# A recurrent attention layer with a gated FFN: the first step's order on four engines, and where the state's products stand in the loop

## The chip, the cores and the metric

The kernel runs on one core of a Trainium2 chip. The metric is the device time of one execution in microseconds (us). The kernel before was run three times: 142.39, 144.08 and 145.32 us, median 144.08 us. A further execution was taken with the profiler; it took 140.76 us, and its span on the core, from the first instruction to the last, is 139.0 us.

## What is computed

For `x` of 4 sequences x 512 tokens x 256 features, with 16 heads of 16:

```
xn   = layernorm(x)
q,k,v = silu(xn Wq), silu(xn Wk), silu(xn Wv)
per head, in chunks:  S_new = chunk_decay * S + (k * k_decay)^T v
                      o     = (q k^T * D) v + (q S) * q_decay
gate = (xn Wg1) Wg2
o    = rmsnorm_per_head(o * sigmoid(gate)) * norm_w
s    = o Wo
g    = silu(fp8(xn * scale) fp8(W2 * scale1) / (scale * scale1))
out  = x + s * g
```

`D` is the causal decay mask. The rounding to 8 bits is done by arithmetic: a magic number derived from the exponent is added and subtracted (`e4_magic`, `e4_sum`, `e4_q`), and values that are too large are turned into NaN by way of PSUM (`find_over`, `put_nan`). W2 goes through the same steps once: `w2_y` (scaled), `w2_m` (exponent), `w2_f32` (magic), `w2_m` (sum), `w2_q`, `w2_over`, `w2_fp8`.

## The kernel before, in words

**Tiling.** The 2048 tokens are worked in 8 steps (`STEPS`). A step `n` takes one tile of 128 tokens from each of two sequences (`S = 2`), so 256 tokens. Steps alternate between two pairs of sequences (`PAIRS = 2`), so the state that step `n` reads was made in step `n - 2`, and steps 0 and 1 begin with a state of zero. A tile of 128 tokens is two chunks of 64 (`c = 0, 1`): `state_mid` is the state between them, `state_end` the state after both. The last two steps make no `state_end`.

**Engines.** Each engine has its own list of instructions, written out by hand, and runs it in order; semaphores tie the lists together. TensorE (PE) has the products, ScalarE (ACT) the silu and tanh functions and copies, VectorE (DVE) the masks, the norms and the states, GpSimd (POOL) the decays and the rounding, SyncE (SP) issues all DMAs. There is no planner: the order in each list is the schedule.

**One step of the loop on PE**, in order (`for n in range(1, STEPS - 1)`, from L1227): `scores(n)` (L1052, 64 small products into `b_s` and `b_o`), `head_sums(n-1)` (L1140), `project_q(n+1)` (L956, L961), `project_g1`, `project_k` and `project_v` of `n+1` (L969 to L998), `spread_rs(n-1)` (L1148), `state_steps(n)` (L1075, 64 products of 64x32: what both chunks add to the state), `gate(n+1)` (L1006), `from_chunk(n,0,0)` (L1116, 32 products), `transpose_x(n+2)`, `from_chunk(n,0,1)`, `transpose_k(n+1)`, `project_o(n-1,0)` (L1164), `from_chunk(n,1,0)`, `from_state(n,0)` and `from_state(n,1)` (L1097, 32 products of 32x32 each: what the state gives to the first and to the second chunk), `ffn(n+1)` (L1023), `from_chunk(n,1,1)`, `project_o(n-1,1)`. The pieces named L1052, L1075, L1097 and L1116 use a part of the array per product (the profile shows it as 32*64, 64*32, 32*32); the others use 128 rows.

**PSUM.** The banks are shared. `ps_u[0]`, where `state_steps` puts the first chunk's share, is in `b_q`; `ps_u[1]`, the second's, is in k's bank `b_k`. `b_o` holds two of the four blocks of scores and then the attention output. `b_v` holds v, and `g1` and `ps_spread` in turn.

**Waits around the change.** `scores(n)` waits for `s_ffn` (the silu of the FFN product of `n`), `s_gate` and `s_og` (`gate_o(n-1)` on DVE, L710). `gate(n+1)` waits for all four masks of step `n` (`mask`, L677). `project_o(n-1,0)` waits for the two states of step `n`. `transpose_k(n+1)` waits for `state_end`.

**The start.** Step 0 stands ahead of the loop in every list. On ACT: ... `silu_q(1)`, `silu_q_parity(1)`, `silu_k(1)`, `normalise(2)`, `silu_v(1)`, `gate(0)`, `high_g1(1)`, `w2_over`, `copy_kT(1)`, `gate(1)`, `find_over(1)`, `high_xT(2)`, `scale_y(2)`, `silu_ffn(0)`, `square_o(0)`, `silu_ffn(1)`. On DVE, near its end: `add_state_mid(0)`, `add_state_end(0)`, `w2_q`, `low_g1(1)`, `head_sum`, `w2_fp8`, `put_nan(1)`, `gate_o(0)`, `low_xT(2)`, `head_spread`, `stats(3)`. POOL scales W2 (L429) and makes its sum (L436).

## Time and profile before

| what | value |
|---|---|
| median of 3 runs | 144.08 us (142.39 to 145.32) |
| the profiled execution | 140.76 us |
| its span | 139.0 us |
| PE busy | 123.4 us, 89% of the span |
| DVE, ACT, POOL busy | 103.3, 75.9, 72.3 us |
| share of PE in the chain that ended last | 66% |

Busy time is the sum over an engine's instructions. A wait says who sat idle before an instruction and what ended it; "issue" means that nothing in the profile explains the idle time. The chain of waits is followed back from the last instruction of all. In the line PEclk each digit is the TensorE clock that was granted in one fortieth of the span, in tenths of full speed.

### The profile page before, as it was taken

What the parts mean: (1) busy time and instruction counts of PE and PEld (TensorE: products, weight loads), DVE (VectorE), ACT (ScalarE), POOL (GpSimd) and SP (SyncE); (2) the same over time, 40 slices, a digit from 0 to 9 for tenths busy, and PEclk for the clock granted to TensorE, in tenths of its full rate; (3) what the DMA queues carried; (4) which work ended last, traced back from release to release, by engine and by line L of the source; (5) the groups of instructions that cost most, each with busy time, mean ns of one, the idle gap of its engine ahead of it and who ended that gap; (6) DMA issues with size and microseconds to landing.
All of it is one profiled execution on the core that took longest, in us unless ns stands there. A gap on an engine that the chain in (4) does not pass through costs nothing.

```text
span 139.0 us, 7207 instructions
## 1 busy us (share of the span) xinstructions
PE 123.4 (89%) x3130; PEld 104.0 (75%) x3130; DVE 103.3 (74%) x276; ACT 75.9 (55%) x143; POOL 72.3 (52%) x112
## 2 busy tenths in 40 slices
PE   3999897945999999999997998999999999887890
PEld 3989895814997799779975896779887987566660
DVE  0899997992888499849990999279937990597963
ACT  7689779829166646664664486365663572104000
POOL 6708999948237186707671584438442842400030
PEclk9999999997799999999999999999999999999999
DMA  2959400000000000100020002000200020020004
GB/s 81 270 155 366 142 0 7 5 0 9 0 0 5 5 5 23 57 5 5 10 73 5 5 0 80 5 5 5 78 5 5 5 78 5 5 80 5 5 0 151
DMA packets 6848, 6.06 MB, mean 44 GB/s; under 512 B 1377, under 2 KB 6817, under 8 KB 6817
## 3 DMA queue, kind: packets, MB, share of 16 engines
q1 hardware_dynamic: 6816, 5.60, 12.6%
q8 instruction: 25, 0.41, 1.2%
q14 instruction: 7, 0.05, 0.1%
HBM read 3.50 MB, written 2.10 MB: 40 GB/s over the span
## 4 chain that ended last, share of the span: by engine, by line
PE 66%; DVE 12%; POOL 10%; issue 8%; ACT 2%; POOLq 0%; DVEq 0%; ACTq 0%
PE b_q L1164 8%; PE b_o L1116 7%; PE b_q L956 5%; PE b_s L1052 4%; PE b_o L1097 4%; PE b_kv L970 4%; PE b_kv L969 4%; PE b_kv L972 4%; PE b_kv L1033 3%; PE b_s L1023 2%; PE b_q L1075 2%; PE b_o L1052 2%; PE b_x L942 2%; PE b_q L961 2%; PE b_s L1006 2%
## 5 line engine op out<-in xcount | busy, mean ns | idle before, releaser
L351 POOL TENSOR_TENSOR e_sum<-e_y,e_magic 128x512 f32<-128x512 f32 x8 | 10.3, 1281 | 19.0 <-DVE e_magic L662 19.0
L710 DVE SCALAR_TENSOR_TENSOR og<-gate_tanh,b_o 128x512 f32<-128x512 f32 x7 | 4.8, 687 | 17.6 <-PE b_o L1116 17.6
L969 PE MATMUL b_kv<-w_hi,xT_hi 128*128 128x256 f32 x64 | 16.6, 281 | 0.0
L970 PE MATMUL b_kv<-w_lo,xT_hi 128*128 128x256 f32 x64 | 16.4, 280 | 0.0
L389 POOL TENSOR_TENSOR y<-sg,x_sb 128x512 f32<-128x512 f32 x7 | 9.0, 1292 | 13.2 <-DVE sg L779 13.2
L1116 PE MATMUL b_o<-probs,v_par 64*32 64x64 f32 x896 | 13.6, 223 | 1.7 <-issue 1.6
L1116 PEld LDWEIGHTS b_o<-probs,v_par 64*32 64x32 f32 x896 | 8.9, 106 | 7.4 <-issue 6.3
L677 DVE TENSOR_TENSOR probs<-b_o,decay_mask 128x512 f32<-128x512 f32 x16 | 10.3, 685 | 4.3 <-PE b_o L1052 4.1
L361 POOL TENSOR_TENSOR qd<-q_silu,q_decay 128x512 f32<-128x512 f32 x8 | 10.4, 1302 | 5.4 <-ACT q_silu L487 5.4
L1164 PE MATMUL b_q<-wo_scaled,on 128*128 128x256 f32 x48 | 13.0, 392 | 0.0
L1052 PE MATMUL b_s<-q_par,kT 32*64 32x128 f32 x256 | 10.1, 293 | 3.1 <-issue 3.1
L972 PE MATMUL b_kv<-w_hi,xT_lo 128*128 128x256 f32 x64 | 12.7, 279 | 0.0
L487 ACT ACTIVATE q_silu<-b_q 128x512 f32<-128x512 f32 x8 | 4.8, 602 | 13.6 <-PE b_q L961 12.9
L1052 PEld LDWEIGHTS b_s<-q_par,kT 32*64 32x64 f32 x256 | 8.1, 139 | 5.5 <-issue 5.4
L969 PEld LDWEIGHTS b_kv<-w_hi,xT_hi 128*128 128x128 f32 x64 | 12.0, 188 | 0.2 <-issue 0.2
L970 PEld LDWEIGHTS b_kv<-w_lo,xT_hi 128*128 128x128 f32 x64 | 12.0, 188 | 0.0
L371 POOL TENSOR_TENSOR own_mid<-state_mid,head_parity 128x128 f32<-128x128 f32 x8 | 3.7, 458 | 15.5 <-DVE state_mid L690 12.8
L1052 PE MATMUL b_o<-q_par,kT 32*64 32x128 f32 x256 | 10.6, 295 | 0.7 <-issue 0.7
L356 POOL TENSOR_TENSOR e_q<-e_sum,e_magic 128x512 bf16<-128x512 f32 x8 | 10.3, 1290 | 0.6
L482 ACT ACTIVATE e_y<-b_x,scales 128x512 f32<-128x512 f32 x8 | 5.5, 689 | 8.8 <-DVE xT_lo L653 8.8
L677 DVE TENSOR_TENSOR probs<-b_s,decay_mask 128x512 f32<-128x512 f32 x16 | 10.2, 680 | 0.0
L492 ACT ACTIVATE q_par<-b_q,head_parity 128x512 f32<-128x512 f32 x16 | 10.1, 688 | 0.0
(184 smaller groups left out, 353.4 us busy)
## 6 DMA issues: line engine op xcount, KB each, us to landing
out_dram<-y SPq DMA_DIRECT2D x7, 256.0 KB, 2.2
x_sb<-in_L_attn_x_dram SPq DMA_DIRECT2D x4, 384.0 KB, 5.7
x_sb<-in_L_attn_x_dram SPq DMA_DIRECT2D x2, 256.0 KB, 3.5
w_f<-in_L_attn_Wq_dram SPq DMA_DIRECT2D x1, 256.0 KB, 3.6
w_f<-in_L_attn_Wk_dram SPq DMA_DIRECT2D x1, 256.0 KB, 3.8
w_f<-in_L_attn_Wv_dram SPq DMA_DIRECT2D x1, 256.0 KB, 4.7
w_f<-in_L_ffn_input_dram SPq DMA_DIRECT2D x1, 256.0 KB, 3.7
wo_f<-in_L_attn_Wo_dram SPq DMA_DIRECT2D x1, 256.0 KB, 6.1
```

Of the source, the lines that this page charges most:

```text
L351: g.tensor_tensor(e4_sum[:], e4_y[:, n % 2], e4_magic[:, n % 2], ALU.add).then_inc(s_e4sum, 1)
L356: g.tensor_tensor(e4_q[:], e4_sum[:], e4_magic[:, n % 2], ALU.subtract).then_inc(s_e4q, 1)
L361: g.tensor_tensor(qd[:, n % 2].rearrange("p k (s t) -> p k s t", s=S), q_silu[:].rearrange("p k (s t) -> p k s t", s=S), q_decay[:].unsque ...
L389: g.tensor_tensor(y[:, n % 2], sg[:, n % 2].rearrange("p (s d) -> p s d", s=S), x_sb[:, x_tiles(n), :], ALU.add).then_inc(s_y, 1)
L492: a.activation(q_par[:, n % 2, par], ps_q, ACT.Silu, scale=head_parity[:, par:par + 1]).then_inc(s_qpar, 1)
L677: v.tensor_tensor(probs[:, r], ps_score[r].rearrange("p (s z) -> p s z", s=S), decay_mask[:, r].unsqueeze(1).broadcast_to([P, S, 4 * C]), ...
L969: t.matmul(dst[:, s], xT_hi[:, u, kk, tok], w_hi[:, w, kk], start=(s == 0 and kk == 0), stop=False, skip_group_check=True)
L970: t.matmul(dst[:, s], xT_hi[:, u, kk, tok], w_lo[:, w, kk], start=False, stop=False, skip_group_check=True)
L972: mm = t.matmul(dst[:, s], xT_lo[:, u, kk, tok], w_hi[:, w, kk], start=False, stop=(kk == KH - 1), skip_group_check=True)
L1052: mm = t.matmul(ps_score[r][c * C:c * C + C, cols], kT[rows, u, half, tok], q_par[rows, u, :, half, tok], start=True, stop=True, skip_grou ...
L1116: mm = t.matmul(dst[32 * r:32 * r + 32, c, z:z + C], v_par[rows, u, blk:blk + 2 * E], probs[rows, r, s, i:i + C], start=(half == 0 and s = ...
L1164: mm = t.matmul(dst, on[:, n % 2, kk, s * P:s * P + P], wo_scaled[:, kk], start=(kk == 0 and (s == 0 or n == STEPS - 1)), stop=(kk == KH - ...
```

## The change

The change has three parts.

1. **The start.** The scaling of W2 moves from POOL to ACT (between `normalise(1)` and `silu_q(0)`), its sum from POOL to DVE. `head_parity` and `own_block` are made at the very start of DVE's list, `head_sum` a little later; the memsets of `wg1_a` and `wg1_b` move behind `lag_logdecay`. SP waits for a lower count before it loads Wg2 and W2. On ACT `silu_q_parity(1)` goes ahead of `silu_q(1)` and `silu_v(1)` ahead of `normalise(2)`. On POOL `decay_k(0)` goes behind the rounding, and `decay_q(1)`, `decay_k(1)` wait for `w2_fp8`. On PE the two FFN products are exchanged: `ffn(1)` comes ahead of `from_chunk(0,1,1)` and `ffn(0)` behind it; ACT takes `silu_ffn(1)` ahead of `scale_y(2)` and `silu_ffn(0)` after `square_o(0)`. `scores(1)` waits for the first of the two only. On DVE `add_state_end(0)`, `stats(3)` and `low_xT(2)` now stand between `put_nan(1)` and `gate_o(0)`.
2. **The state's steps.** `state_steps(n)` is cut in two calls of 32 products. The first, `c = 0`, stays in its place. The second, `c = 1`, comes behind `transpose_x(n+2)`, writes to v's bank `b_v` instead of `b_k`, waits for `silu_v(n+1)`, and stands where `from_chunk(n,0,1)` stood; that one and `transpose_k(n+1)` come behind `project_o(n-1,0)`. `project_g1` now waits for `state_end`, `transpose_k` and `project_o` no longer do.
3. **The state's share.** `from_state(n,0)` goes between `project_k(n+1,0)` and `project_k(n+1,1)`, waits for the first mask, and begins the sum in the bank's first half; `from_state(n,1)` stays.

Before the last step, `state_steps(7)` moves ahead of `from_chunk(6,1,1)`.

```diff
@@ -160,7 +160,7 @@
 ps_ffn0 = b_q[:].rearrange("p (s n) -> p s n", s=S)
-ps_u = [b[:, 0:W // 4].rearrange("p (k s e) -> p k s e", k=KH, s=S) for b in (b_q, b_k)]
+ps_u = [b[:, 0:W // 4].rearrange("p (k s e) -> p k s e", k=KH, s=S) for b in (b_q, b_v)]
 ps_k = b_k[:].rearrange("p (s n) -> p s n", s=S)
...
@@ -413,34 +415,34 @@
 pool.wait_ge(s_pool, 11)
-g.memset(wg1_a[:].bitcast(F32), 0.0).then_inc(s_pool, 1)
-g.memset(wg1_b[:].bitcast(F32), 0.0).then_inc(s_pool, 1)
 g.memset(head_sum[:], 0.0).then_inc(s_pool, 1)
...
 g.memset(minus_third[:], 0.0).then_inc(s_pool, 1)
-pool.wait_ge(s_pool, 16)
+pool.wait_ge(s_pool, 14)
 g.memset(minus_third[64:96], -1.0).then_inc(s_pool, 1)
+pool.wait_ge(s_pool, 15)
+pool.wait_ge(s_laglog, 1)
+g.memset(wg1_a[:].bitcast(F32), 0.0).then_inc(s_pool, 1)
+g.memset(wg1_b[:].bitcast(F32), 0.0).then_inc(s_pool, 1)
 pool.wait_ge(s_pool, 17)
 norm_factors(1)
-pool.wait_ge(s_w2, 16)
-pool.wait_ge(s_scale[1], 16)
-g.tensor_scalar(w2_y[:], w2_f32[:], scales[:, 1:2], None, ALU.mult).then_inc(s_w2q, 1)
-decay_k(0)
 sum_y(0)
 round_y(0)
+decay_k(0)
 decay_q(0)
 norm_factors(2)
-pool.wait_ge(s_w2q, 3)
-g.tensor_tensor(w2_m[:], w2_y[:], w2_f32[:], ALU.add).then_inc(s_w2sum, 1)
 sum_y(1)
-pool.wait_ge(s_dvec, 4)
+pool.wait_ge(s_hpar, 2)
 own_state_mid(0)
 round_y(1)
-own_state_end(0)
+pool.wait_ge(s_w2q, 6)
 decay_q(1)
 decay_k(1)
+own_state_end(0)
 norm_factors(3)
@@ -524,7 +526,8 @@
 def silu_ffn(n):
-    act.wait_ge(s_ffnps, n + 1)
+    act.wait_ge(s_ffnps, 2 - n if n < 2 else n + 1)
     need(act, s_sg, n - 2)
...
@@ -574,21 +577,25 @@
 normalise(1)
+act.wait_ge(s_w2, 16)
+act.wait_ge(s_scale[1], 16)
+a.activation(w2_y[:], w2_f32[:], ACT.Copy, scale=scales[:, 1:2]).then_inc(s_w2q, 1)
 silu_q(0)
-act.wait_ge(s_wg2, 64)
-a.activation(wg2_hi[:], wg2_f32[:], ACT.Copy).then_inc(s_g2w, 1)
 act.wait_ge(s_vzero, 2)
...
 high_g1(0)
+act.wait_ge(s_wg2, 64)
+a.activation(wg2_hi[:], wg2_f32[:], ACT.Copy).then_inc(s_g2w, 1)
 scale_y(1)
 find_over(0)
+act.wait_ge(s_qps, 2)
+silu_q_parity(1)
 silu_q(1)
-silu_q_parity(1)
 silu_k(1)
+silu_v(1)
 normalise(2)
-silu_v(1)
 gate(0)
@@ -597,11 +604,11 @@
 high_xT(2)
+act.wait_ge(s_dvec, 4)
+silu_ffn(1)
 scale_y(2)
-act.wait_ge(s_dvec, 6)
+square_o(0)
 silu_ffn(0)
-square_o(0)
-silu_ffn(1)
 act.wait_ge(s_wo, 48)
...
@@ -695,6 +703,7 @@
     p = pair(n)
+    dve.wait_ge(s_u[1], n + 1)
     dve.wait_ge(s_mid, mids(n))
...
@@ -783,9 +792,14 @@
+dve.wait_ge(s_pool, 9)
+v.tensor_reduce(head_parity[:, 0:1], own_head[:].rearrange("p (a b) -> p a b", b=2)[:, :, 0], AX_X, ALU.add).then_inc(s_hpar, 1)
+v.tensor_tensor(own_block[:], own_head[:].rearrange("p (a b) -> p a b", b=2)[:, :, 0],
+                own_head[:].rearrange("p (a b) -> p a b", b=2)[:, :, 1], ALU.add)
+dve.wait_ge(s_hpar, 1)
+v.tensor_scalar(head_parity[:, 1:2], head_parity[:, 0:1], -1.0, 1.0, ALU.mult, ALU.add).then_inc(s_hpar, 1)
 stats(0)
 dve.wait_ge(s_ld, 16)
-dve.wait_ge(s_pool, 9)
 for half in range(KH):
@@ -797,6 +811,11 @@
 v.tensor_scalar(not_ahead[:], lag[:], 0.0, None, ALU.is_ge).then_inc(s_ahead, 1)
+dve.wait_ge(s_pool, 12)
+for half in range(KH):
+    hs = v.tensor_scalar(head_sum[:, half].rearrange("p (j z) -> p j z", j=8)[:, :, half * HH:half * HH + HH],
+                         own_head[:].unsqueeze(1).broadcast_to([P, 8, HH]), 0.5, None, ALU.mult)
+hs.then_inc(s_hsum, 1)
 dve.wait_ge(s_w[0], 16)
...
@@ -837,41 +851,39 @@
     mask(0, r)
+dve.wait_ge(s_w2q, 1)
+v.tensor_scalar(w2_m[:].bitcast(I32), w2_y[:].bitcast(I32), 0x7F800000, None, ALU.bitwise_and).then_inc(s_w2q, 1)
 low_xT(1)
...
 dve.wait_ge(s_g2w, 1)
-dve.wait_ge(s_pool, 17)
+dve.wait_ge(s_pool, 15)
 v.scalar_tensor_tensor(out=wg2_stack[:], in0=wg2_hi[:].bitcast(F32), scalar=minus_third[:, 0:1], in1=wg2_f32[:],
...
 magic(1)
-dve.wait_ge(s_w2q, 1)
-v.tensor_scalar(w2_m[:].bitcast(I32), w2_y[:].bitcast(I32), 0x7F800000, None, ALU.bitwise_and).then_inc(s_w2q, 1)
 dve.wait_ge(s_w2q, 2)
 v.tensor_scalar(w2_f32[:], w2_m[:], E4_MIN, E4_MAGIC, ALU.max, ALU.mult).then_inc(s_w2q, 1)
+dve.wait_ge(s_w2q, 3)
+v.tensor_tensor(w2_m[:], w2_y[:], w2_f32[:], ALU.add).then_inc(s_w2sum, 1)
 put_nan(0)
 add_state_mid(0)
-add_state_end(0)
 dve.wait_ge(s_w2sum, 1)
...
 v.reciprocal(inv_scales[:], scales[:]).then_inc(s_dvec, 1)
-for half in range(KH):
-    hs = v.tensor_scalar(head_sum[:, half].rearrange("p (j z) -> p j z", j=8)[:, :, half * HH:half * HH + HH],
-                         own_head[:].unsqueeze(1).broadcast_to([P, 8, HH]), 0.5, None, ALU.mult)
-hs.then_inc(s_hsum, 1)
-dve.wait_ge(s_dvec, 5)
+dve.wait_ge(s_dvec, 3)
 v.tensor_scalar(descale[:], inv_scales[:, 0:1], inv_scales[:, 1:2], None, ALU.mult).then_inc(s_dvec, 1)
...
 put_nan(1)
+add_state_end(0)
+stats(3)
+low_xT(2)
 gate_o(0)
-low_xT(2)
 dve.wait_ge(s_pec, 1)
 v.tensor_scalar(head_spread[:], ps_spread, -0.75, None, ALU.mult).then_inc(s_dvec, 1)
-stats(3)
 exponent(2)
@@ -888,8 +900,8 @@
     add_state_mid(n)
+    put_nan(n + 1)
     add_state_end(n)
-    put_nan(n + 1)
     if known(n + 3):
@@ -949,7 +961,7 @@
-        pe.wait_ge(s_ffn, 1)
+        pe.wait_ge(s_ffn, 2)
     for part in (w_hi, w_lo):
@@ -990,8 +1002,11 @@
     pe.wait_ge(s_v, n if n > 1 else n + 1)
+    if n > 1:
+        pe.wait_ge(s_end, min(n - 1, STEPS - PAIRS))
     if n == 2:
-        pe.wait_ge(s_dvec, 7)
+        pe.wait_ge(s_dvec, 5)
     for kk in range(KH):
...
@@ -1026,8 +1041,6 @@
     pe.wait_ge(s_k, n + 1)
-    need(pe, s_end, min(n, STEPS - PAIRS))
     for s in range(S):
@@ -1039,7 +1052,7 @@
     if n > 0:
-        pe.wait_ge(s_ffn, n + 1 if n < STEPS - 1 else n)
+        pe.wait_ge(s_ffn, 1 if n == 1 else n + 1 if n < STEPS - 1 else n)
         pe.wait_ge(s_gate, n + 1)
@@ -1053,28 +1066,32 @@
-def state_steps(n):
+def state_steps(n, c):
     u = n % 2
+    if c == 1 and pos(n) == NB - 1:
+        return
     pe.wait_ge(s_kd, n + 1)
     pe.wait_ge(s_v, n + 1)
-    pe.wait_ge(s_kT, n + 1)
     if known(n + 1):
-        pe.wait_ge(s_k, n + 2)
-        pe.wait_ge(s_qpar, 2 * (n + 2))
+        if c == 0:
+            pe.wait_ge(s_q, n + 2)
+            pe.wait_ge(s_qpar, 2 * (n + 2))
+        else:
+            pe.wait_ge(s_v, n + 2)
+        dst = ps_u[c]
     else:
...
         pe.wait_ge(s_on, n - 1)
-    u_ps = ps_u if known(n + 1) else [ps_u_last]
+        dst = ps_u_last
     for half in range(KH):
...
             for r in range(4):
-                for c in range(2 if pos(n) < NB - 1 else 1):
-                    rows = slice(c * C, c * C + C)
-                    heads = v_par[rows, u].rearrange("p (q z) -> p q z", q=2)[:, :, 0:W].rearrange("p q (a z) -> p a q z", a=H)
-                    mm = t.matmul(u_ps[c][32 * r:32 * r + 32, half, s], kd[rows, u, s, half * P + 32 * r:half * P + 32 * r + 32],
-                                  heads[:, s * HH + half * 4 + r, :, 0:E], start=True, stop=True, skip_group_check=True)
-    mm.then_inc(s_u, 1)
+                rows = slice(c * C, c * C + C)
+                heads = v_par[rows, u].rearrange("p (q z) -> p q z", q=2)[:, :, 0:W].rearrange("p q (a z) -> p a q z", a=H)
+                mm = t.matmul(dst[32 * r:32 * r + 32, half, s], kd[rows, u, s, half * P + 32 * r:half * P + 32 * r + 32],
+                              heads[:, s * HH + half * 4 + r, :, 0:E], start=True, stop=True, skip_group_check=True)
+    mm.then_inc(s_u[c], 1)
...
@@ -1095,10 +1114,9 @@
                 t.matmul(dst[rows, c, z:z + C], st, qd[rows, u, half, s * P + c * C:s * P + c * C + C],
-                         start=(last and half == 0 and s == 0), stop=False, skip_group_check=True)
+                         start=((c == 0 or last) and half == 0 and s == 0), stop=False, skip_group_check=True)
 def from_chunk(n, half, s):
@@ -1115,7 +1133,7 @@
                               probs[rows, r, s, i:i + C],
-                              start=(half == 0 and s == 0 and par == 0 and not last),
+                              start=(half == 0 and s == 0 and par == 0 and not last and (c == 1 or pos(n) == 0)),
                               stop=(par == 1), skip_group_check=True)
@@ -1155,7 +1173,6 @@
             pe.wait_ge(s_mid, mids(n + 1))
-            pe.wait_ge(s_end, ends(n + 1))
         elif n == STEPS - 2:
@@ -1204,7 +1221,7 @@
 project_v(1, 1)
-state_steps(0)
+state_steps(0, 0)
 pe.wait_ge(s_g2w, 2)
@@ -1213,16 +1230,21 @@
 transpose_x(2)
+pe.wait_ge(s_g1lo, 2)
+state_steps(0, 1)
 from_chunk(0, 1, 0)
 from_state(0, 1)
+pe.wait_ge(s_w2q, 6)
+ffn(1)
 from_chunk(0, 1, 1)
+ffn(0)
 pe.wait_ge(s_hsum, 1)
+pe.wait_ge(s_end, 1)
 for half in range(KH):
...
 mm.then_inc(s_pec, 1)
-pe.wait_ge(s_w2q, 6)
-ffn(0)
-ffn(1)
@@ -1230,28 +1252,30 @@
     project_k(n + 1, 0)
+    from_state(n, 0)
     project_k(n + 1, 1)
...
     spread_rs(n - 1)
-    state_steps(n)
+    state_steps(n, 0)
     gate(n + 1)
...
         transpose_x(n + 2)
-    from_chunk(n, 0, 1)
-    transpose_k(n + 1)
+    state_steps(n, 1)
     if n == 1:
...
     project_o(n - 1, 0)
+    from_chunk(n, 0, 1)
+    transpose_k(n + 1)
     from_chunk(n, 1, 0)
-    from_state(n, 0)
-    from_state(n, 1)
     if known(n + 2):
+        from_state(n, 1)
         ffn(n + 1)
+    else:
+        from_state(n, 1)
+        state_steps(n + 1, 0)
     from_chunk(n, 1, 1)
-    if not known(n + 2):
-        state_steps(n + 1)
     project_o(n - 1, 1)
```

## Rows read from the trace of the kernel before

**Rows 1.** The page: granted TensorE clock in 40 slices, and the instruction queue (packets, MB).
```profile
PEclk9999999997799999999999999999999999999999
q8 instruction: 25, 0.41, 1.2%
```

**Rows 2.** Who waited for whom, on PE: us in total, times, longest us.
```profile
PE b_s L1052 <- issue: 3.1, 1, 3.1
PE b_o L1116 <- issue: 1.6, 2, 1.0
```

**Rows 3.** The chain of waits: start us, us, what; where each `scores` begins.
```profile
32.94 0.35 PE b_s L1052 x2
...
47.98 0.26 PE b_s L1052 x2
...
62.02 0.26 PE b_s L1052 x2
...
92.09 0.26 PE b_s L1052 x2
...
106.04 0.26 PE b_s L1052 x2
...
119.57 0.26 PE b_s L1052 x2
```

**Rows 4.** The timeline (start us, us, what, idle before) of ACT, 20 to 34 us.
```profile
22.93 0.61 ACT L512 ACTIVATE v_par<-b_kv 128x512 f32<-128x512 f32 x1
...
26.71 0.61 ACT L499 ACTIVATE b_s<-e_q 128x512 f32<-128x512 bf16 x1
...
30.37 0.69 ACT L482 ACTIVATE e_y<-b_x,scales 128x512 f32<-128x512 f32 x1 [2.54 <-DVE xT_lo L653]
...
32.05 0.69 ACT L530 ACTIVATE ffn_silu<-b_s,descale 128x512 f32<-128x512 f32 x1
```

**Rows 5.** The timeline of DVE, 23 to 32 us.
```profile
23.44 0.47 DVE L701 SCALAR_TENSOR_TENSOR state_end<-state_mid,chunk_decay,b_kv 128x64 f32<-128x64 f32 x2
...
26.73 1.69 DVE L868 SCALAR_TENSOR_TENSOR w_fp<-w_over,w_q 128x512 bf16<-128x512 bf16 x1
28.45 0.69 DVE L667 SCALAR_TENSOR_TENSOR xqT<-b_s,e_q 128x512 bf16<-128x512 f32 x1
29.06 0.68 DVE L710 SCALAR_TENSOR_TENSOR og<-gate_tanh,b_o 128x512 f32<-128x512 f32 x1
29.66 0.68 DVE L653 TENSOR_TENSOR xT_lo<-b_x,xT_hi 128x512 fp32r<-128x512 f32 x1
...
30.59 0.74 DVE L643 BATCH_NORM_STATS2 bn<-x_sb 128x6 f32<-128x256 f32 x2
```

**Rows 6.** The timeline of PE at 22 us, where `state_steps(0)` begins.
```profile
22.33 0.19 PE L1075 MATMUL b_q<-v_par,kd 64*32 64x32 f32 x1 [0.81 <-ACT k_nat L505]
```

**Rows 7.** The timeline of POOL, 13 to 28 us.
```profile
13.08 1.58 POOL L429 TENSOR_SCALAR w_y<-w_f,scales 128x512 f32<-128x512 f32 x1
...
26.60 1.28 POOL L361 TENSOR_TENSOR qd<-q_silu,q_decay 128x512 f32<-128x512 f32 x1
```

**Rows 8.** The timeline of DVE in step 3: the last two masks.
```profile
67.87 1.28 DVE L677 TENSOR_TENSOR probs<-b_s,decay_mask 128x512 f32<-128x512 f32 x2
```

**Rows 9.** The timeline of PE in step 6: the gate's products.
```profile
113.28 0.47 PE L1006 MATMUL b_s<-g1T,wg_stack 128*128 128x256 f32 x2 [0.23 <-issue]
```

**Rows 10.** The chain of waits: pieces of steps 1, 3 and 6 on PE.
```profile
45.42 0.58 PE b_o L1097 x32
...
68.40 0.23 PE b_x L1148 x2
...
69.32 0.43 PE b_s L1006 x2
...
72.94 1.03 PE b_o L1097 x64
...
118.17 0.34 PE b_x L1075 x29
```

More of the change, by code:

```diff
@@ L195, in layer_kernel @@
         s_hsum = sem("head_sum_ready")
+        s_hpar = sem("head_parity_ready")
         s_whi = [sem(f"w{name}_hi_ready") for name in "qkv"]
@@ L243, in layer_kernel @@
         s_probs = sem("probs_ready")
-        s_u = sem("state_steps_in_psum")
+        s_u = [sem(f"state_steps_{c}_in_psum") for c in range(2)]
         s_mid = sem("state_mid_ready")
@@ L306, in _ @@
             sp.dma_start(wg1_f32[:], Wg1.rearrange("(k p) n -> p k n", p=P)).then_inc(s_wg1, 16)
-            sp.wait_ge(s_pool, 15)
+            sp.wait_ge(s_pool, 13)
             for r in range(4):
@@ L365, in decay_k @@
                 pool.wait_ge(s_k, n + 1)
-                need(pool, s_u, n - 1)
+                need(pool, s_u[0], n - 1)
+                need(pool, s_u[1], min(n - 1, STEPS - PAIRS))
                 g.tensor_tensor(kd[:, n % 2].rearrange("p s (h e) -> p s h e", h=H), k_nat[:].rearrange("p s (h e) -> p s h e", h=H),
@@ L568, in _ @@
             act.wait_ge(s_qps, 1)
-            act.wait_ge(s_dvec, 4)
+            act.wait_ge(s_hpar, 2)
             silu_q_parity(0)
@@ L665, in put_nan @@
                 dve.wait_ge(s_over, n + 1)
-                need(dve, s_ffnps, n - 1)
+                need(dve, s_ffnps, n - 1 if n != 2 else 2)
                 v.scalar_tensor_tensor(out=xqT[:, n % 2].rearrange("p k t -> p (k t)"), in0=ps_over, scalar=0.0, in1=e4_q[:],
@@ L682, in add_state_mid @@
                 u_ps = ps_u if n < STEPS - 1 else [ps_u_last]
-                dve.wait_ge(s_u, n + 1)
+                dve.wait_ge(s_u[0], n + 1)
                 need(dve, s_ownmid, n - PAIRS + 1)
@@ L776, in product @@
                 dve.wait_ge(s_outps, S * (n + 1))
-                dve.wait_ge(s_ffn, n + 1)
+                dve.wait_ge(s_ffn, max(n + 1, 2))
                 need(dve, s_y, n - 1)
@@ L808, in _ @@
                             ld_units[:].unsqueeze(2).broadcast_to([P, H, C]), ALU.mult).then_inc(s_laglog, 1)
-            v.tensor_reduce(head_parity[:, 0:1], own_head[:].rearrange("p (a b) -> p a b", b=2)[:, :, 0], AX_X, ALU.add).then_inc(s_dvec, 1)
-            dve.wait_ge(s_dvec, 3)
-            v.tensor_scalar(head_parity[:, 1:2], head_parity[:, 0:1], -1.0, 1.0, ALU.mult, ALU.add).then_inc(s_dvec, 1)
             low_xT(0)
@@ L822, in _ @@
             low_w(2)
-            v.tensor_tensor(own_block[:], own_head[:].rearrange("p (a b) -> p a b", b=2)[:, :, 0],
-                            own_head[:].rearrange("p (a b) -> p a b", b=2)[:, :, 1], ALU.add)
             dve.wait_ge(s_wg1, 16)
-            dve.wait_ge(s_pool, 14)
+            dve.wait_ge(s_pool, 17)
             g1_cols = slice(0, 96)
@@ L1013, in ffn @@
                     pe.wait_ge(s_qpar, 4)
-                    pe.wait_ge(s_end, 1)
+                    pe.wait_ge(s_mid, 1)
                 else:
@@ L1087, in from_state @@
                     pe.wait_ge(s_ownend, ends(n - PAIRS))
+                    if not last:
+                        pe.wait_ge(s_probs, 4 * n + 1)
                 else:
```

## Prediction, made before the changed kernel was built or run

> **What bounds the kernel now.** I read four views. The waits of PE come first: PE is busy for nearly all of the span, so the question is where it is not. Two entries stand out [rows 2]: one gap of 3.1 us ahead of `scores` (L1052), and two gaps inside `from_chunk` (L1116) that add up to 1.6 us. Second, the chain of waits gives the start of every `scores`, so the length of every step [rows 3]: step 1 takes 47.98 - 32.94 = 15.04 us, step 2 takes 14.04, steps 3 and 4 together 30.07, step 5 takes 13.95, step 6 takes 13.53. Steps 3 and 4 are 2.0 us longer than two steps of 14.04; that is where the two gaps of [rows 2] lie, and I price one at 1.0. Otherwise a step is PE at work from end to end, plus one wait that the page hides: the gate's products wait for the last mask. DVE ends it at 67.87 + 1.28 = 69.15, and the gate starts at 69.32 [rows 8, 10], just when `state_steps` is through too. In step 6, where `state_steps` has only 32 products, PE reaches the gate early and sits idle for 0.23 us [rows 9]. So up to the gate two paths are equally long, 69.32 - 62.02 = 7.3 us; from the gate on, PE alone counts, 14.04 - 7.3 = 6.7 us.
>
> Third, the timelines of ACT and DVE around the 3.1 us. `scores(1)` starts at 32.94, behind `silu_ffn(1)`, which runs 32.05 to 32.74 [rows 3, 4]. That one stands behind `scale_y(2)`, which waited 2.54 us for `low_xT(2)` on DVE [rows 4], which stood behind `put_nan(1)` (28.45) and `gate_o(0)` (29.06) [rows 5]. `put_nan(1)` starts as `w2_fp8` ends, 26.73 + 1.69 = 28.42 [rows 5]. Fourth, the clock: it is near full speed in every slice but the two behind this gap, which show 7 tenths [rows 1], between the levels of 1.2 and 2.4 GHz. Step 1 is 1.0 us longer than step 2.
>
> **Part 1, the start.** Step by step:
> - `state_steps(0)` came 0.81 us after PE was free, because ACT made `k_nat` last [rows 6]; now it waits for q's silus, which come first. PE goes on at 21.5.
> - `silu_v(1)` ran at 22.93 behind `normalise(2)` [rows 4]. Ahead of it, it can start as v's products end, at about 21.6: 1.3 us earlier. `normalise(2)` now stands between it and the gate's tanh and takes back about 0.5, so the chain through `high_g1(1)` and `gate(1)` to `find_over(1)`, which ran at 26.71 [rows 4], gains 0.8 (1.3 to 0.3): it runs at 25.9.
> - `w2_fp8` took 1.69 us, while other VectorE operations of 128x512 take 0.69 [rows 5]; POOL's `qd` ran from 26.60 to 27.88 beside it [rows 7]. POOL is now held until it is done, so I give it 0.7. The scaling of W2 cost POOL 1.58 us at 13.08 [rows 7]; ACT does such an operation in at most 0.69 (`scale_y` [rows 4]) and has waits behind it in this stretch. DVE gets the sum, 0.7 at most, and loses `head_sum` from this stretch. I count the two as hidden; uncovered, they cost 0.7 each. That DVE makes `head_parity` and `own_block` while it waits for x I count as nothing either way, and the loads of Wg2 and W2 come no later, since SP waits for less.
> - `put_nan(1)` then starts at 25.9 + 0.6 = 26.5 instead of 28.45.
> - What is late next: `gate_o(0)`. Behind `put_nan(1)` (0.6) there now stand `add_state_end(0)` (0.45), `stats(3)` (0.74 for the first part and an estimated 0.25 for its second) and `low_xT(2)` (0.6), then `gate_o(0)` itself (0.7) [rows 5]: 26.5 + 0.6 + 0.45 + 1.0 + 0.6 + 0.7 = 29.85. `scores(1)` waits for it, and starts at about 29.9 instead of 32.94: **3.0 us gained**. `silu_ffn(1)`, which it also waits for, is done by 28.5, since `ffn(1)` follows `put_nan(1)` directly.
> - PE's longest gap before `scores(1)` is then some 0.9 us. Gaps of this size stand ahead of `state_steps(0)` [rows 6] and in steps 3 and 4 [rows 2], and the clock stayed at 9 tenths there [rows 1]. So step 1 should run at full speed: **1.0 gained**.
>
> **Parts 2 and 3, the loop.** Nothing is taken away; 32 products of `from_state(n,0)` and 32 of `state_steps(n)` move. Price list [rows 10]: `from_state` takes 1.03 for 64 products and 0.58 for 32 alone, so the second 32 cost 0.45 in company. Two products of 128 rows behind their own kind take 0.23 (L1148); the gate's two, between groups of small products, take 0.43 (L1006). So going into small products and back costs 0.20. `state_steps` took 69.32 - 68.63 = 0.69 for 64; 29 alone took 0.34, so 32 take 0.38.
> - Up to the gate, steps 2 to 5: `from_state(n,0)` between the halves of k costs 0.45 + 0.20 = 0.65, the cut of `state_steps` gives back 0.69 - 0.38 = 0.31. PE comes 0.34 later than the masks, which no longer count.
> - From the gate on: -0.45 for `from_state(n,0)`, +0.38 for `state_steps(n,1)`, and +0.2 for one more island of small products (`from_chunk(n,0,1)` between `project_o` and `transpose_k`); 0.1 of this is inside the 0.38. So about +0.05.
> - Per step +0.4, four steps: **+1.6**. Step 1 has no `from_state(1,0)` and keeps the masks' 7.3, but gets `state_steps(1,1)`, +0.4 to +0.5 over step 6's 13.5: so 14.0, as counted above. Step 6: +0.65 less the 0.23 that it waited, -0.45 and +0.2 behind the gate: **+0.1**.
> - The waits that are added: `from_state(n,0)` for the first mask, which DVE has done 2 us before; `project_g1` for `state_end` of the step before; `state_steps(n,1)` for `silu_v(n+1)`, which ACT ends about 0.6 before PE gets there. I count none. If the last did bind, `project_o` and all behind it would wait with it.
>
> On the price of an island, the Trainium skill ("TensorEngine Tiling (Array Packing)", Key Properties) speaks against this change: changing the tiling mode drains the engine. It gives no time. The trace agrees that there is a price, and its 0.20 us is what the sum uses; without the rule's drain the loop would cost 0.2 x 2 x 4 = 1.6 less, so nothing.
>
> **The two gaps in `from_chunk`.** Nothing in the profile ends them, and they lie in the middle of 32 like products. The instruction queue moved 25 packets of 16 KB [rows 1]; I take the gaps for instructions that come late where PE uses them fastest. The old order has `from_chunk`, `from_state` twice, `ffn`, `from_chunk` in one run, the new one spreads them: `from_state(n,0)` out, 128-row products between the chunks. What this is worth no row shows: it lies between both gaps gone (-2.0) and a gap in each of six steps (+4.0). I take one of two gone, **-1.0**: the stretches get thinner, but the densest one (`from_chunk`, `from_state`, `from_chunk`) keeps 96 of its 128 small products. The Trainium skill ("Runtime: NRT & Kernel Launch", Instruction fetch mechanics) says the cost of crossing a 16 KiB block is mostly hidden. By it the gaps would have another cause, and the change would leave them; the sum would then be 1.0 higher.
>
> **Sum.** -3.0 - 1.0 + 1.6 + 0.1 - 1.0 = -3.3. The profiled execution of 140.76 us becomes 137.5 (span 139.0 becomes 135.7). The median of the runs shown is 3.32 above the profiled one, and the sum says nothing of that; 144.08 - 3.3 = **140.8 us**, 2.3% less. About 2% is what a measurement of this kernel can tell from no change.
>
> **Rivals.**
> 1. *The gaps go altogether.* For it: the densest stretch is broken up. -4.3: 139.8 us.
> 2. *The gaps stay, and switches are dear.* An island may cost up to the whole 0.43 of the gate instead of 0.20: two per step, four steps, +1.8 at most. Both gaps stay: -2.3 + (0 to 1.8): 141.8 to 143.6 us. For it: the rule on draining.
> 3. *`gate_o(0)` stays late.* If `find_over(1)` or `w2_fp8` does not get earlier, `put_nan(1)` stays near 28 and the new 2.0 us between it and `gate_o(0)` eat the gain; `scores(1)` starts at 31.4: -1.5 instead of -3.0. 142.3 us.
> 4. *The other side: a gap in every step.* The new order may put fast stretches where blocks end, for instance at `state_steps(n,0)` and `from_chunk`. Six gaps of 1.0 instead of two: -2.3 + 4.0 = +1.7, 145.8 us. It decides from five gaps on (2.3 over what there is). Against it: three of five like steps have none now.
>
> **Chances.** Forecast 0.35, rival 1 0.20, rival 2 0.22, rival 3 0.15, rival 4 0.08. The range takes the start from 1.6 to 3.8, the loop from +0.8 to +2.6, the gaps from -2.0 to 0: 144.08 - 1.6 - 0.5 + 2.6 = 144.6 at one extreme, 138.1 at the other; both together are unlikely, and I take 138.0 to 143.9. Faster by over 2% means below 141.2: two thirds of the forecast (0.24), nearly all of rival 1 (0.19), a fifth of rivals 2 and 3 (0.08): 0.51. Slower by over 2% (above 147.0) is a tail of rival 4, 0.03; within 2% 0.46.
>
> **What would show it.** `put_nan(1)` starts near 26.5, `gate_o(0)` ends near 29.8, `scores(1)` starts near 29.9 with PEclk at 9 after it; step 1 takes 14.0, steps 2 to 5 take 14.4 without gaps, step 6 13.6. In the loop the gate starts 7.6 us after `scores`, and no longer right behind a mask. The forecast is wrong if `scores(1)` starts after 31, if step 2 takes more than 14.8, or if gaps named "issue" of about 1 us stand in more than two steps.

## The result, and the profile after

| | before | after |
|---|---|---|
| median of the runs | 143.24 us (141.56 to 145.32, 4 runs) | 136.33 us (135.97 to 136.70, 4 runs) |
| ratio of the runs, 95% interval | | 0.960 (0.953 to 0.967) |
| the profiled execution, its span | 140.76, 139.0 us | 136.16, 134.4 us |

The changed kernel is 4.0% faster. The forecast of 140.8 us had the direction right and the size wrong: 6.9 us of median where 3.3 were forecast, outside the range. A ratio leaves out runs more than 1.5% above their kernel's fastest, so it can differ from the ratio of the medians, above all for kernels whose runs are spread.

The chain of waits of the changed kernel (start us, us, what), where each `scores` begins. It answers to [rows 3].

```profile
29.54 0.33 PE b_s L1065 x2
...
43.73 0.26 PE b_s L1065 x2
...
58.27 0.26 PE b_s L1065 x2
...
72.89 0.26 PE b_s L1065 x2
...
87.44 0.26 PE b_s L1065 x2
...
102.00 0.26 PE b_s L1065 x2
...
115.48 0.25 PE b_s L1065 x2
```

Against [rows 3]: `scores(1)` is 3.4 us earlier; step 1 takes 14.19 instead of 15.04 (0.85 less), step 2 14.54 instead of 14.04 (0.5 more), steps 3 and 4 together 29.17 instead of 30.07 (0.9 less), step 5 14.56 instead of 13.95 (0.6 more), step 6 13.48 instead of 13.53. From `scores(7)` to the end of the span it is 18.9 instead of 19.4. In sum -3.4 - 0.85 + 0.5 - 0.9 + 0.6 - 0.05 - 0.5 = -4.6 us, the difference of the spans.

The waits on PE in the changed kernel (us in total, times, longest us) answer to [rows 2]. The 3.1 us ahead of `scores` have become 0.5 and end with `gate_o`'s `og`; the gaps in the loop's `from_chunk` are gone. What is left of "issue" at L1134 stands behind `scores(7)`.

```profile
PE b_s L1065 <- DVE og L719: 0.5, 1, 0.5
...
PE b_kv L1134 <- issue: 0.4, 1, 0.4
```

The timeline of DVE at the end of the first step, which answers to [rows 5], and the granted clock in 40 slices, which answers to [rows 1].

```profile
24.90 0.68 DVE L879 SCALAR_TENSOR_TENSOR w_fp<-w_over,w_q 128x512 bf16<-128x512 bf16 x1
26.25 0.69 DVE L675 SCALAR_TENSOR_TENSOR xqT<-b_s,e_q 128x512 bf16<-128x512 f32 x1 [0.68 <-ACT b_s L501]
26.86 0.47 DVE L710 SCALAR_TENSOR_TENSOR state_end<-state_mid,chunk_decay,b_kv 128x64 f32<-128x64 f32 x2
27.24 0.75 DVE L650 BATCH_NORM_STATS2 bn<-x_sb 128x6 f32<-128x256 f32 x2
...
28.12 0.67 DVE L660 TENSOR_TENSOR xT_lo<-b_x,xT_hi 128x512 fp32r<-128x512 f32 x1
28.71 0.68 DVE L719 SCALAR_TENSOR_TENSOR og<-gate_tanh,b_o 128x512 f32<-128x512 f32 x1
```
```profile
PEclk9999999999999999999999999999999999999998
```

One whole step, number 2, in the chain of waits of the changed kernel, from `from_state(2,0)` on. The gate (L1021) comes 51.50 - 43.73 = 7.8 us after `scores`, where it was 7.3 [rows 10], and no mask ends just ahead of it.

```profile
48.00 0.58 PE b_o L1116 x32
...
51.12 0.39 PE b_q L1092 x32
51.50 0.43 PE b_s L1021 x2
...
52.91 0.39 PE b_kv L1092 x32
```

### The profile page after: what moved, and what is told of

It is laid out like the page before. It is cut to its first block, busy times and chain, and to the rows that moved or that the text cites. A ratio compares the mean times of both kernels' runs of the same rounds, so it can differ in the third digit from the quotient of the medians.

```text
span 134.4 us, 7213 instructions
## 1 busy us (share of the span) xinstructions
PE 124.6 (93%) x3130; PEld 103.8 (77%) x3130; DVE 101.2 (75%) x277; ACT 77.3 (57%) x144; POOL 69.0 (51%) x110
## 4 chain that ended last, share of the span: by engine, by line
PE 82%; DVE 7%; issue 5%; ACT 4%; POOL 1%; POOLq 0%; DVEq 0%; ACTq 0%
PE b_q L1181 9%; PE b_o L1134 7%; PE b_q L968 7%; PE b_kv L981 7%; PE b_kv L984 6%; PE b_kv L982 6%; PE b_s L1065 5%; PE b_o L1116 5%; PE b_s L1187 4%; PE b_q L973 3%; PE b_kv L1046 3%; PE b_x L954 3%; PE b_o L1065 2%; PE b_s L1038 2%; PE b_s L1021 2%
## 5 line engine op out<-in xcount | busy, mean ns | idle before, releaser
L981 PE MATMUL b_kv<-w_hi,xT_hi 128*128 128x256 f32 x64 | 17.1, 290 | 0.0
L1181 PE MATMUL b_q<-wo_scaled,on 128*128 128x256 f32 x48 | 13.5, 404 | 0.1
L1134 PE MATMUL b_o<-probs,v_par 64*32 64x64 f32 x896 | 13.1, 222 | 0.2 <-issue 0.2
L1134 PEld LDWEIGHTS b_o<-probs,v_par 64*32 64x32 f32 x896 | 8.7, 106 | 5.6 <-issue 4.6
L373 POOL TENSOR_TENSOR own_mid<-state_mid,head_parity 128x128 f32<-128x128 f32 x8 | 3.6, 455 | 17.7 <-DVE state_mid L698 14.8
L1065 PE MATMUL b_o<-q_par,kT 32*64 32x128 f32 x256 | 10.0, 280 | 0.0
L984 PEld LDWEIGHTS b_kv<-w_hi,xT_lo 128*128 128x128 f32 x64 | 9.8, 188 | 0.0
```

The source lines that it names most:

```text
L981: t.matmul(dst[:, s], xT_hi[:, u, kk, tok], w_hi[:, w, kk], start=(s == 0 and kk == 0), stop=False, skip_group_check=True)
L984: mm = t.matmul(dst[:, s], xT_lo[:, u, kk, tok], w_hi[:, w, kk], start=False, stop=(kk == KH - 1), skip_group_check=True)
L1065: mm = t.matmul(ps_score[r][c * C:c * C + C, cols], kT[rows, u, half, tok], q_par[rows, u, :, half, tok], start=True, stop=True, skip_grou ...
L1134: mm = t.matmul(dst[32 * r:32 * r + 32, c, z:z + C], v_par[rows, u, blk:blk + 2 * E], probs[rows, r, s, i:i + C], start=(half == 0 and s = ...
L1181: mm = t.matmul(dst, on[:, n % 2, kk, s * P:s * P + P], wo_scaled[:, kk], start=(kk == 0 and (s == 0 or n == STEPS - 1)), stop=(kk == KH - ...
```

## The experiments

"Old loop" means parts 2 and 3 undone. All times are medians; the kernel before was run beside each, with medians between 142.6 and 143.4 us. The rounds ran on different chips, so times of different rounds are compared with that in mind.

**Which part does it: four kernels on one chip.**

`start_only`, the changed start with the old loop:

```
- ps_u in (b_q, b_v); state_steps(n, 0) ... state_steps(n, 1)
+ ps_u in (b_q, b_k); state_steps(n), add_state_end(0) behind add_state_mid(0)
- project_k(n+1, 0); from_state(n, 0); project_k(n+1, 1)
+ from_chunk(n, 1, 0); from_state(n, 0); from_state(n, 1)
```

> The first step as changed, the loop as before (parts 2 and 3 undone; add_state_end(0) stands where it stood, since the state's second share is in k's bank again). Theory A, the start gave 3.4 us up to scores(1) and 0.85 in step 1, and the loop's two parts took away the gaps inside from_chunk, of which the timed runs before had more than the profiled one: 138.5 to 139.5 us against 143.2, gaps named issue of 0.5 us or more still in the loop, steps without one 14.0 us. Theory B, the start did it all: 136.3 us or less, no such gaps.

Measured: 137.22 us, four runs from 135.11 to 138.53. By the gaps theory A is borne out. By the time neither is: 137.22 lies between the two. Its waits on PE:

```profile
PE b_o L1124 <- issue: 2.0, 2, 1.7
```

The longer gap ended at 82.63 us. The windows of this kernel around it (us, PE busy and number, granted clock, DMA share, GB/s) show what one gap can set off: from 82.7 to 86.1 us, 3.4 us long, the clock stood at half, 1.2 GHz, and this step took 89.35 - 71.88 = 17.5 us instead of 14.1.

```profile
81.00:82.00 1.00, 0.00 (x0) 1.00 0.06 11
82.00:83.00 1.00, 0.37 (x11) 0.85 0.01 5
83.00:84.00 1.00, 1.00 (x9) 0.50 0.05 16
86.00:87.00 1.00, 1.00 (x84) 0.94 0.00 0
```

`loop_only`, parts 2 and 3 with the old start:

```
- the lists of POOL, ACT, DVE and PE for step 0 as changed
+ as before, but add_state_end(0) just ahead of put_nan(1), and own_state_end(0) behind decay_k(1)
```

> The loop as changed (parts 2 and 3), the first step's lists as before but for add_state_end(0), which waits for the second call of state_steps. Theory A: no gaps over 0.5 us in the loop, steps 2 to 5 take 14.5 us each, the stall of about 3 us ahead of scores(1) and the lower clock behind it stay; 140 to 141 us against 143.2. Theory B: 143.2 or above, since the steps are 0.5 us longer each and the gaps had gone by the start.

Measured: 142.53 us, ten runs from 142.24 to 143.51; the kernel before beside it 142.97, thirteen runs from 140.79 to 146.2. The ratio, 1.007 (1.002 to 1.011), puts it no lower than the kernel before. It has no gap of 0.3 us or more in the loop, as theory A said, but PE now waits for `add_state_end(0)` before it transposes `head_sum`, and that is a new wait:

```profile
29.83 0.52 PE L1234 MATMUL b_kv<-ident,head_sum 128*128 128x128 f32 x2 [1.65 <-DVE state_end L706]
```

`scores(1)` came at 34.08, 1.1 later than before, and step 1 took 16.6 us, with the clock at half from 30.0 to 40.2 us. So its time is no clean price of the loop; its small spread is the finding.

`start_steps`, the start and part 2 alone (`from_state(n,0)` back beside `from_state(n,1)`):

> The start and part 2 (state_steps in two calls, the second in v's bank), from_state(n,0) back beside from_state(n,1). Theory A with part 2 as what thins the stretches: 136 to 137 us, no gap, steps of 14.2 us. If it is part 3 that takes the gaps away: gaps stay, 138 to 139.5.

Measured: 137.23 us (136.78 to 137.98). Steps 1 to 6 took 14.0, 14.7, 15.4, 14.5, 14.8 and 13.6 us, with one gap of 0.31. Part 2 thins the loop, but it does not pay: `start_only` had 137.22. Without part 3 its four runs still lie within 1.2 us.

`start_share`, the start and part 3 alone (`state_steps` in one call, in k's bank):

> The start and part 3 (from_state(n,0) between the halves of k), state_steps in one call again. If part 3 takes the gaps away: 136 to 137 us and steps 2 to 5 at 14.2 to 14.4; if it is part 2: gaps of about 1 us stay in two or more steps, 138 to 140 us.

Measured: 134.80 us (133.57 to 135.08), ratio to the kernel before 0.949 (0.936 to 0.962). Its median is 1.5 lower than that of the change itself, though the intervals of the two ratios overlap; it was run again below. Its longest gap in the loop up to `scores(7)` is 0.37 us, in step 2. The chain gives its steps:

```profile
29.50 0.32 PE b_s L1061 x2
...
43.05 0.26 PE b_s L1061 x2
57.94 0.25 PE b_s L1061 x2
72.21 0.26 PE b_s L1061 x2
86.48 0.26 PE b_s L1061 x2
```

Step 1 takes 13.55 us, step 2 14.89, steps 3 and 4 take 14.27. Step 2 is thus 0.62 longer for a gap of 0.37: the products around a gap come slower too, and the gap that is shown is less than what is lost. The changed kernel takes 14.19 and 14.6: part 2 costs 0.6 in step 1 and 0.3 in the others.

**What the gaps are.** `start_only_shift` puts 32 more products in front of `scores(1)` of `start_only`:

```
+ for _ in range(32):
+     matmul(ps_score[1][:, 0:8], ident, ident[:, 0:8])
```

> The kernel with the changed start and the old loop, with 32 more products of 8 columns on PE ahead of scores(1) (their result is not used). If the gaps are instructions that come late in blocks of 256, they stand again at matmul counts 1601, 1852, 2859 and 2984, so 32 matmuls earlier in the program than before: not in the from_chunk where they stood, and their sum changes with the place. If they belong to the work at that place (a wait, a bank), they stay at the same line and the counts become 1633 and 1884.

Measured: 146.53 us. The added products took 8.7 us, so the time says nothing; the places do. The windows below are cut at the ends of the gaps; the number behind PE busy counts matmuls. First the kernel before, then `start_only`, then `share_by_steps` (below), then this one.

```profile
0.00:75.89 75.89, 67.53 (x1601) 0.98 0.18 56
75.89:86.86 10.97, 10.34 (x251) 1.00 0.08 27
86.86:121.34 34.48, 33.48 (x1007) 1.00 0.06 19
```
```profile
0.00:70.57 70.57, 66.41 (x1601) 1.00 0.20 60
70.57:82.62 12.05, 10.34 (x251) 1.00 0.08 24
82.62:118.33 35.71, 35.18 (x1007) 0.95 0.06 19
```
```profile
0.00:53.55 53.55, 48.74 (x1097) 1.00 0.24 73
53.55:67.74 14.19, 13.71 (x378) 1.00 0.07 23
67.74:82.53 14.79, 13.73 (x377) 1.00 0.07 21
82.53:116.96 34.43, 33.99 (x1007) 1.00 0.06 20
```
```profile
0.00:123.17 123.17, 118.01 (x2860) 0.97 0.14 42
123.17:126.89 3.72, 3.11 (x125) 1.00 0.02 5
126.89:130.71 3.82, 2.32 (x127) 1.00 0.22 73
```

In all four the gaps that PE has in the loop, from 0.3 us up, stand on one grid of matmul counts with a pitch of 126, to within one: 251 is 2 of it, 377 is 3, 1007 is 8, and 1097, 1601, 1852 and 2859 lie on it. With its weight load each matmul is two instructions, so 126 matmuls and some waits make 256. In the shifted kernel, whose added products count 64 matmuls, the gap at 2860 stands in `project_o`, no longer in `scores(7)`. But I had expected gaps at 1601 and 1852 too, and there were none: with this work at those counts the loop ran in steps of 14.1 to 14.2 us. The traces say what differs. The 126 matmuls ahead of 1601 and 1852 took 2.4 and 2.8 us in the kernel before and in `start_only`, 3.7 and 6.7 here, and 3.7 and 4.4 in `start_share`. So a boundary is needed, and dense work ahead of it too.

The trace also shows the instructions arrive, which settles what the gaps are. The 25 packets of 16 KB of the instruction queue are in its DMA records; 3130 matmuls at 126 to a block are 24.8 blocks. In the kernel before, the packet in front of count 1601 runs from 73.55 to 74.47 us; PE falls idle at 74.89 and goes on at 75.90. In the shifted kernel, at count 2860, it runs from 120.66 to 121.88; PE falls idle at 121.88 and goes on at 123.18. A window of the DMA view over the first of the two (73.5 to 74.5 us in the kernel before) holds nothing else:

```profile
DMA packets 1, 0.02 MB, mean 16 GB/s; under 512 B 0, under 2 KB 0, under 8 KB 0
q8 instruction: 1, 0.02, 5.8%
```

The 17 traces of this case have 40 gaps of 0.25 us or more at boundaries from count 1097 on, those at 3112 left out that an operation of VectorE ends. After every one of the 40, PE goes on 1.0 to 1.6 us after a packet has landed. At the 218 boundaries there with less than 0.1 us of gap the first matmul comes at least 1.1 us after its packet too (at one of them a second packet had landed just before it, and the earlier one is counted). A packet takes 0.9 to 1.9 us, and in front of the gaps of 1 us and more it started 1.0 to 1.6 us after PE had crossed the boundary before. So a block that PE works off in under 3 us can leave it waiting for the next. It need not: in the changed kernel the 126 matmuls ahead of 1601 took 2.84 us, but the packet had started 0.2 us ahead of the boundary before, and there is no gap. The Trainium skill ("Runtime: NRT & Kernel Launch", Instruction fetch mechanics) says instructions are fetched in blocks of 256, and that crossing a block is mostly hidden. The trace agrees with the first; for the second the measurement decides: most boundaries show no gap, but with small products ahead of one, 0.3 to 1.7 us are not hidden.

`start_only_nostore` asks whether the stores hold the blocks up:

```
- for n in range(STEPS - 1): ... dma_start(out_v[...], y[...])
+ only for n == STEPS - 2 (the output of steps 0 to 5 is left out)
```

> The changed start and the old loop, without the stores of steps 0 to 5 (that part of the output is left out). If the stores hold up the blocks of instructions, the gaps in the loop go or shrink below 0.3 us and the runs lie within 0.6 us of each other near 133.5 us; if density alone makes them, they stay near 1 us and the runs stay spread over 2 us or more.

Measured: 135.75 us (135.25 to 136.36). The gaps are there all the same:

```profile
PE b_o L1122 <- issue: 1.9, 3, 1.1
```

The stores do not make them, but one can lengthen a gap. At count 1852 the packet took 1.86 us in `start_only`, where a store shared the DMA engines with it, and the gap was 1.70; in `start_only_again` (below) 1.65 and 1.45, a store beside it too; here, with none, 1.27 and 1.12. The runs lie closer together than those of `start_only`; with four runs each I leave that open.

`share_by_steps` moves `from_state(n,0)` of `start_share` next to the other small products:

```
- project_k(n+1, 0); from_state(n, 0); project_k(n+1, 1)
+ spread_rs(n-1); from_state(n, 0); state_steps(n)
```

> The changed start, state_steps in one call, from_state(n,0) directly ahead of state_steps(n) instead of between the halves of k: no island of its own, but 96 small products in one stretch. If an island costs 0.2 us, steps 2 to 5 take 14.05 us instead of the 14.27 of the version with it between the halves; if the density makes the gaps, one of 0.5 us or more stands in or behind state_steps, and the median is at or above 134.8 us. Without gaps 133.8 us.

Measured: 137.15 us (136.09 to 138.93), 2.3 above `start_share`, which ran in another round; the intervals of the ratios overlap, and the profiled executions differ by 1.4. The same instructions in the same number, 32 of them elsewhere. Step 5 has no gap and takes 14.1 us, so the island costs 0.2. Steps 2 to 4 take 15.2 to 15.3 us each, 2.3 more in all than in `start_share`, with these gaps at the grid's boundaries:

```profile
53.56 0.27 PE L1042 MATMUL b_kv<-ident,k_nat 128*128 128x128 f32 x1 [0.91 <-issue]
...
67.75 0.41 PE L1126 MATMUL b_o<-probs,v_par 64*32 64x64 f32 x19 [0.48 <-issue]
...
82.54 0.31 PE L1126 MATMUL b_o<-probs,v_par 64*32 64x64 f32 x6 [0.95 <-issue]
```

**The kernel before again, and part 3 alone on it.**

> The kernel before, once more with the profiler. Theory A: its gaps vary from run to run and the first profiled execution (140.76 us against a median of 143) was one with few of them; this one shows the same steps of 14.04 us where there is no gap, but gaps at matmul counts of the same grid (1097, 1475, 1601, 1852, 2859 ...) whose sum in the loop differs from 2.0 us by as much as the whole time differs from 140.76. Theory B: the time above the profile lies elsewhere, gaps of 2.0 us as before.

Measured: median 142.39 us, eight runs from 140.63 to 144.82, and it was the profiled one that took 140.63. Its gaps in the loop add up to 1.7 us, at the same places as in the first. So theory A was not shown this way: both profiled executions of this kernel are about 2 us below its median, and no trace says what the others spent.

`share_only` is the kernel before with part 3 and nothing else:

> The kernel before with from_state(n,0) between the halves of k and nothing else (start and state_steps as before). Theory A: steps 2 to 5 cost 0.23 us more each and the gaps behind from_state go: 140.5 to 141.5 us against 142.9, runs within 1 us of each other. Theory B (gaps do not hang on the order of the loop): 143.8.

Measured: 140.63 us, ten runs, nine from 139.99 to 141.07 and one of 138.80; its profiled execution took 140.65. The kernel before beside it: 142.59, nineteen runs from 139.94 to 145.32. The medians differ by 2.0 us, in favour of theory A, but the ratio, 0.996 (0.989 to 1.003), does not tell the two apart, and the profiled executions are equal. Here the median is the time of the profiled execution. Its step 1 took 14.9 us and its steps 3 to 5 took 14.27.

**The pieces of the start**, each undone alone in the changed kernel.

`ffn_in_order`:

```
- ffn(1); from_chunk(0,1,1); ffn(0)   |  silu_ffn(1) ... square_o(0), silu_ffn(0)
+ ffn(0); from_chunk(0,1,1); ffn(1)   |  silu_ffn(0) ... square_o(0), silu_ffn(1)
```

> The changed kernel with the exchange of the two FFN products alone undone: ffn(0) first, ffn(1) behind from_chunk(0,1,1), scores(1) waits for both silus. If gate_o(0) is what scores(1) waits for, ffn(1)'s silu ends at about 30.6 behind square_o(0), so scores(1) starts at 30.7 instead of 29.54: 1.2 us longer, 137.5 us. If the exchange does nothing, 136.3.

Measured: 138.96 us (137.28 to 140.75), 2.6 more, twice what I expected.

```profile
30.93 0.32 PE L1065 MATMUL b_s<-q_par,kT 32*64 32x128 f32 x2 [2.30 <-issue]
```
```profile
PEclk9999999995999999999999999999999999999999
```

`scores(1)` is 1.4 later, as worked out, but the wait of 2.3 us in one piece is followed by a slice of half the clock, and step 1 takes 15.4 us instead of 14.2.

`no_hold`, `pool.wait_ge(s_w2q, 6)` left out:

> The changed kernel without POOL's hold for w2_fp8, so decay_q(1) runs beside it. If the two contend as before, w2_fp8 takes 1.3 to 1.7 us instead of 0.68, put_nan(1) starts at 26.6 or later instead of 26.25 and scores(1) 0.3 to 0.7 us later than 29.54: 136.6 to 137.0 us. If the hold does nothing: 136.3.

Measured: 136.22 us, so no difference. DVE's `w2_fp8` still took 0.68 us, from 24.66; POOL's `decay_q(1)` started at the same moment and took 1.82 us instead of 1.27:

```profile
24.66 1.82 POOL L362 TENSOR_TENSOR qd<-q_silu,q_decay 128x512 f32<-128x512 f32 x1
```

`w2_on_pool`, `w2_y` back on POOL ahead of `sum_y(0)`:

> The changed kernel with the scaling of W2 back on POOL (ahead of sum_y(0)). POOL's list is then 1.5 us later, so the rounding of step 0 and decay_q(0) hold silu_q(1) and the FFN of step 0; exponent and magic take twice as long beside it. scores(1) 0.5 to 1.5 us later than 29.54: 136.8 to 137.8 us. If POOL had slack: 136.3.

Measured: 137.58 us (137.26 to 137.78), 1.25 more. `scores(1)` starts at 30.12, 0.6 later; the rest is step 1 (14.39) and single steps further on.

**The three loops once more, with more runs, on one chip.**

> The changed start and part 3 only, state_steps in one call: 134.8 us, 1.5 below the changed kernel, runs within 1 us of each other. If the 1.5 was the chip and not part 2, it equals the changed kernel within 0.4 us.

> The changed kernel: 136.3 us, all runs within 0.8 us of each other, and 6.4 to 6.9 below the kernel before.

> The changed start with the old loop: runs spread over 2 us or more around 137.2 us, 2.0 to 2.4 above start_share_again, as share_only stood 2.0 below the kernel before. If the spread does not hang on the loop's order, it spreads as little as the other two.

| kernel | median | runs | ratio to before, interval |
|---|---|---|---|
| start_share_again | 134.86 | 133.58 to 135.81 (6) | 0.941 (0.934 to 0.948) |
| after_again | 136.14 | 134.96 to 137.27 (6) | 0.950 (0.943 to 0.957) |
| start_only_again | 136.99 | 135.76 to 139.82 (6) | 0.955 (0.948 to 0.962) |

The order of the three is that of the first round. The intervals of the first two still overlap, by 0.005, so that part 2 costs 1.3 rests on both rounds together and on the lengths of the steps. `start_only` spreads over 4.1 us, the others over 2.2 and 2.3, more than I expected of them. Against `start_only`, `start_share` is 2.1 lower, and its interval ends where the other begins; the changed kernel lies between. The profiled execution of `start_only_again` took 139.82 us and has gaps of 1.45 and 1.45 us at the known places. Behind the first, which ended at 72.09, the clock stood at half from 72.5 to 75.9; behind the second it did not fall. Its granted clock in 40 slices:

```profile
PEclk9999999999999999999995999999999999999999
```

## Why the prediction was wrong

1. **The start up to `scores(1)`: right.** Forecast 29.9, measured 29.54. `put_nan(1)` came at 26.25 (forecast 26.5) and waited for `find_over(1)`, as worked out; `gate_o(0)` ended at 29.39 (29.85), and it is what `scores(1)` waits for. The reason given for `w2_fp8` was wrong in part: `no_hold` shows that POOL's hold is not needed, since here the two start at the same moment, where VectorE's started 0.13 us behind GpSimd's before, and it is GpSimd's that takes longer.
2. **Step 1: right.** Forecast 14.0 at full clock, measured 14.19, with PEclk at 9 in every slice of the step. `start_share` and `share_only` split it: with the gap gone and its half clock with it the step goes from 14.9 to 13.55, 1.4 less, and part 2 takes 0.6 of that back. `ffn_in_order` shows the other side: the exchange of the FFN products is worth 1.4 us of waiting and 1.2 of clock. That a gap of about 1 us leaves the clock alone held here (PE's longest, ahead of `scores(1)`, was 0.54), but of the two gaps of 1.45 one was followed by half the clock, and the one of 1.70 in `start_only` too.
3. **The loop: right in its making, somewhat too cheap.** Forecast +0.4 a step, measured 0.5 in step 2, the same in steps 3 and 4 and 0.6 in step 5 against 14.04 and 13.95 without gaps: 7.8 us up to the gate (forecast 7.6) and 6.8 behind it (6.75). An island costs 0.2, as forecast (`share_by_steps`: 14.08 against 14.27).
4. **The gaps: the term that was mis-sized.** The sum took one gap of two as gone, -1.0. In the trace both went, -2.0, and the stretch from `scores(7)` on, which I had not counted, gave another 0.5. That is luck as far as the traces tell: it took 18.4 us in the second profiled execution of the kernel before and 19.7 in that of the changed one. So -1.0 here, -0.5 behind `scores(7)`, -0.4 in point 1, and +0.6 for the dearer loop make the profiled execution 4.6 us faster instead of 3.3; steps 1 and 6 cancel. What I took the gaps for, instructions that come late, was right, and their packets show it.
5. **The step that failed: "the sum says nothing of that".** I carried the 3.3 us by which the median stood above the profiled execution over to the changed kernel. With the 4.6 us of the trace in place of 3.3 the forecast would have been 139.5, still 3.2 above 136.33. Some 4.4 us lie between forecast and result: 1.3 are the sum's; 0.8 are the median of the kernel before, 144.08 in three runs and 143.24 in four; 2.3 are the excess that did not carry over. The kernel before has medians 1.8 to 2.6 us above its two profiled executions, by the run, and the changed kernel has 0.2 or less. That the forecast was too small does not hang on this excess: the ratio of 0.953 to 0.967 means 4.7 to 6.7 us of 143.24, and the traces alone give 4.6.

What the excess is stays open, but the unprofiled runs narrow it down, for each has its mean granted clock on record. Of the 59 runs of the kernel before in the rounds of experiments, 20 have 0.983 to 0.988, with a median of 141.8 us; 28 have 0.970 to 0.976, median 143.1; 11 have 0.964 or 0.965, median 145.2. All ten runs of the changed kernel, and all ten of `start_share`, have 0.994 or more. Of the ten runs of `start_only`, the four from 0.985 to 0.988 have a median of 138.0, the other six 136.2. So the slower runs spent more time at half the clock, and the traces show such stretches behind gaps and waits of 1.45 us and more. The clock is not all of it: the second profiled execution of the kernel before took only 140.63 at 0.975, since 2 us of its half clock fell into the wait ahead of `scores(1)`, and in `share_only` the runs at 0.972 to 0.975 are as fast as those at 0.983 to 0.988, within 0.3 us.

That the new place of `from_state(n,0)` takes the excess away is likely, not shown. `share_only` and `start_share` have none and `start_only` spreads wide, but the ratio of `share_only` does not set it apart from the kernel before, and `start_steps`, without part 3, has 0.5 and a small spread. The traces do show that gaps at the same two counts in the same program vary, 0.29 and 1.70 us in one execution of `start_only`, 1.45 and 1.45 in another.

By the medians the start is worth 5.8 us (`start_share` 134.80 against `share_only` 140.63), not 4.0. The traces give 4.9: 3.5 up to `scores(1)` and 1.4 in step 1; the stretch from `scores(7)` on, where two executions of `start_share` differ by 1.1, adds between 0 and 1. Part 3 is worth some 2.0 by the medians (140.63 against 142.59, and 134.86 against 136.99), and part 2 takes back 1.3 to 1.5 (136.14 against 134.86, and 136.33 against 134.80). These lie along one chain of kernels, so that they add up, -5.8 - 2.0 + 1.4 = -6.4, proves nothing; side by side 6.9 and 7.2 were measured (143.24 against 136.33, 143.35 against 136.14).

Of the rivals, the first (all gaps gone, 139.8) had the mechanism right; the second had switching too dear; the third (`gate_o(0)` late) did not come; the fourth (new gaps) came in `share_by_steps`, not in the change. The rule on draining (Trainium skill, "TensorEngine Tiling (Array Packing)", Key Properties) fits the 0.2 us an island costs.
